# Two cross-attention layers on one Trainium2 core: projections issued in two steps, the first layer's last output chunk packed, orders and PSUM banks laid out anew

## The reference

```python
# layer 0 (its branch for tokens after the 77th is empty)
q, k, v = x @ Wq.T, ctx @ Wk.T, ctx @ Wv.T                 # split in 20 heads
x = merge(softmax(q @ k.T / 4) @ v) @ Wo.T + bo + x
# layer 1
q, k, v = x @ W_q, text @ W_k, text @ W_v                  # text: 73 tokens
p = softmax(q @ k.T / 4)
qsem = l2norm(p @ text)                                     # 512 wide, per head
sem = qsem @ l2norm(ip).T                                   # ip: 4 image tokens
p_ip = softmax(q @ k_ip.T / 4 + 0.5 * sem) * mask
x = merge(p @ v + p_ip @ v_ip) @ W_out + b_out + x
```

## Time and profile of the kernel before

| | us |
|---|---|
| median of three timed runs | 2387.35 |
| lowest and highest of them | 2387.01, 2389.14 |
| profiled execution, its own time | 2386.11 |
| profiled execution, span of the instructions | 2384.3 |
| of it, the first stage, about | 330 |
| period of the second stage | 30.76 |

### The profile page before, as it was taken

How to read it: one execution, slowest core, us unless ns; L and a number is a source line. 1 busy time by engine, 2 the same in 40 slices (tenths; PEclk the granted TensorE clock), 3 DMA queues, 4 the chain that set the end, 5 groups by cost and what they waited for, 6 DMA issues and landing times.

```text
span 2384.3 us, 85416 instructions
## 1 busy us (share of the span) xinstructions
PE 2201.3 (92%) x32824; PEld 1392.7 (58%) x32824; DVE 1832.2 (77%) x3453; ACT 1699.4 (71%) x2604; POOL 1591.4 (67%) x1056
## 2 busy tenths in 40 slices
PE   7999967999999999999999999999999999999984
PEld 5777744555555555555555555555555555555542
DVE  6856634888888888888888888888888888888873
ACT  4333316878888877888888888887888788888862
POOL 4131225777777777777777777777777777777762
PEclk9999978999999999999999999999999999999997
DMA  8877642444444444444444444444444444444431
GB/s 274 268 225 214 203 128 57 116 120 121 120 120 119 122 116 114 118 117 123 119 122 120 116 121 120 121 122 120 119 117 121 114 118 118 123 119 122 120 88 58
DMA packets 338300, 310.57 MB, mean 130 GB/s; under 512 B 180224, under 2 KB 281856, under 8 KB 337920
## 3 DMA queue, kind: packets, MB, share of 16 engines
q1 hardware_dynamic: 337920, 305.36, 45.4%
HBM read 164.66 MB, written 105.98 MB: 114 GB/s over the span
## 4 chain that ended last, share of the span: by engine, by line
PE 46%; POOL 15%; ACT 10%; issue 9%; DVE 4%; DMA 1%; SPq 0%; ACTq 0%; DVEq 0%; POOLq 0%
PE psum L1011 17%; PE psum L1096 8%; POOL e L1439 8%; ACT ef L1207 8%; PE psum L1114 8%; POOL ust L1401 5%; PE psum L1075 3%; PE psum L1014 3%; POOL al L1406 2%; PE psum L1037 2%; PE psum L1126 2%; PE psum L1051 1%; DVE x1b L1371 1%; ACT q_high L1189 1%; DVE x1a L1371 1%
## 5 line engine op out<-in xcount | busy, mean ns | idle before, releaser
L1439 POOL TENSOR_TENSOR e<-ef,eh 73x1024 f32<-73x1024 f32 x320 | 679.7, 2132 | 207.9 <-PE psum L1126 126.6
L1207 ACT ACTIVATE ef<-psum 73x1024 f32<-73x1024 f32 (+1 forms) x640 | 635.4, 1013 | 66.2 <-PE psum L1079 66.0
L1269 DVE TENSOR_REDUCE mneg<-psum 128x8 f16<-128x616 f32 (+3 forms) x512 | 451.0, 934 | 9.6 <-PE psum L1037 1.0
L1296 DVE TENSOR_TENSOR e<-psum,e 73x1024 f32<-73x1024 f32 x320 | 384.6, 1202 | 10.1 <-PE psum L1114 5.7
L1114 PE MATMUL psum<-eh,gram 128*73 128x512 f16 x1280 | 336.8, 386 | 42.8 <-DVE mneg L1269 14.3
L1096 PE MATMUL psum<-ef,values 128*32 128x256 f32 x5120 | 361.8, 387 | 0.4
L1222 ACT ACTIVATE eh<-ef 73x1024 f16<-73x1024 f32 x320 | 337.0, 1054 | 7.4
L1215 ACT ACTIVATE ust<-psum 128x512 f32<-128x512 f32 x384 | 226.5, 595 | 127.4 <-POOL al L1406 116.2
L1401 POOL TENSOR_TENSOR ust<-ust,rb 128x768 f32<-128x768 f32 x128 | 232.2, 1814 | 86.0 <-DMA rb<-r_dram 85.9
L1406 POOL TENSOR_TENSOR al<-ust,ah 128x768 f16<-128x768 f32 x128 | 210.2, 1642 | 85.8 <-ACT ah L1247 85.8
L1276 DVE SCALAR_TENSOR_TENSOR q_low<-psum,q_high 128x640 f16<-128x640 f32 x128 | 105.5, 824 | 201.6 <-ACT q_high L1189 194.5
(11 more groups left out here) (188 smaller groups left out, 4790.5 us busy)
## 6 DMA issues: line engine op xcount, KB each, us to landing
rb<-r_dram SPq DMA_DIRECT2D x128, 384.0 KB, 3.8
keys<-k_dram SPq DMA_DIRECT2D x128, 231.0 KB, 3.8
values<-v_dram SPq DMA_DIRECT2D x128, 192.5 KB
ust<-ust SPq DMA_DIRECT2D x512, 48.0 KB, 2.4
v_dram<-vst SPq DMA_DIRECT2D x64, 320.0 KB
out<-outt SPq DMA_DIRECT2D x64, 320.0 KB, 2.2
k_dram<-kst SPq DMA_DIRECT2D x32, 616.0 KB, 3.7
x<-in_x SPq DMA_DIRECT2D x32, 384.0 KB, 5.0
```

The costliest lines, as they stand in the source:

```text
L1207: act.activation(ef[l][0:m, unit_heads(n), :].rearrange("t h s -> t (h s)"), src, ACT.Exp, scale=SM).then_inc(s_exp[l], 1)
L1269: dve.tensor_reduce(dst, o, AX_X, ALU.max, negate=True).then_inc(s_max[l], 1)
L1296: dve.tensor_tensor(rest, banks(l, f"u{k}", 2)[0:m, :, :], rest, ALU.mult).then_inc(s_wr, 1)
L1439: pool.tensor_tensor(e2[0:m, k, :, :], ef[1][0:m, unit_heads(k), :], eh[0:m, unit_heads(k), :], ALU.subtract).then_inc(s_e2, 1)
```

## The change

`q` and `o` of both layers become two steps each, on all engines that touch them: part 0 is chunks 0 and 1 (512 columns, one bank), part 1 is the last chunk (128 columns, in a bank of its own). The steps need not stand together any more, and the semaphores count two per batch. Layer 0's last output chunk is packed like the others; DVE writes the two halves with two instructions, and a new SP step `xd` copies each half to the other 64 partitions with one transfer each, which POOL's `xh` of layer 1 waits for. Later steps of layer 1's output lag one batch more. `ORDER` and `USES` are written anew for all engines.

```diff
+PARTS = ((0, 1), (2,))
 ORDER = {
     "pe": """
-        1u2/3 1a1/3 0t1/1 1q/2 0t2/1 0a0/1 1s0/2 0a1/1 1s1/2 0a2/1 1i/2 1a2/3 1u3/3 1m/2 1u4/3 1t0/2 0q/0 1n0/3 1n1/3
-        1n2/3 1p/4 1u0/2 1n3/3 1n4/3 0s0/0 1a0/2 0s1/0 1u1/2 1t1/2 1o/4 1t2/2 0m/0 1y/3 0o/1 0t0/0""",
+        0a1/1 0t2/1 1q0/2 0a2/1 1s0/2 1q1/2 1a2/3 1s1/2 0q0/0 1m/2 1o1/5 1t0/2 1u4/3 1p/4 1n0/3 0s0/0 1n1/3 0q1/0
+        1t1/2 1u0/2 1n2/3 1n3/3 1n4/3 0s1/0 1o0/4 1t2/2 1u1/2 0m/0 1u2/2 1y/3 0t0/0 0o0/1 0o1/1 1u3/2 0a0/0 0t1/0 1i/2
+        1a0/2 1a1/2""",
     "act": """
-        0t0/1 0t1/1 1h4/3 1a1/3 0t2/1 1f/4 0t3/1 1q/2 0t4/1 0a0/1 1r/3 0a1/1 0a2/1 1i/2 1a2/3 1m/2 0r/1 1t0/2 1h0/2
-        1t1/2 0q/0 1h1/2 1g/4 1n/3 1a0/2 0g/1 1t2/2 1t3/2 1h2/2 1t4/2 0m/0 1h3/2""",
+        1a0/3 1i/3 1a1/3 0a1/1 1f/4 0t4/1 1q0/2 0a2/1 1q1/2 0r/0 1a2/3 1m/2 0q0/0 1t0/2 1t1/2 1h0/2 1h1/2 1g/4 0q1/0
+        1t2/2 1t3/2 1h2/2 1n/3 1h3/2 0g/1 1t4/2 0m/0 1r/3 0t0/0 0t1/0 1h4/2 0a0/0 0t2/0 0t3/0""",
     "dve": """
-        1y7/4 1y8/4 1y9/4 1y10/4 1y11/4 1w2/3 1y12/4 1y13/4 1y14/4 1y15/4 1y16/4 1y17/4 1y18/4 1ql/2 1tw0/2 1s0/2
-        1s1/2 1s2/2 1s3/2 1tw1/2 1w3/3 0d/1 1w4/3 0ql/0 1p/4 1w0/2 0s0/0 0s1/0 0s2/0 0s3/0 1w1/2 0tw0/0 1d/3 0tw1/0
-        1o/4 1y0/3 1y1/3 1y2/3 1y3/3 1y4/3 1y5/3 1y6/3 0o/1""",
+        1y9/4 1y10/4 1y11/4 1y12/4 1y13/4 1y14/4 1y15/4 1y16/4 1y17/4 1y18/4 1ql0/2 1s0/2 1s1/2 1s2/2 1s3/2 1tw0/2
+        1tw1/2 0d/1 1ql1/2 0ql0/0 1o1/5 1w4/3 1p/4 0s0/0 0s1/0 0tw0/0 1w0/2 0ql1/0 0tw1/0 0s2/0 0s3/0 1o0/4 1w1/2 1d/3
+        1y0/3 1y1/3 1y2/3 0o0/1 0o1/1 1w2/2 1y3/3 1w3/2 1y4/3 1y5/3 1y6/3 1y7/3 1y8/3""",
     "pool": """
-        1xh/2 1xl/2 1vb/4 1b3/3 0xh/0 1at/4 0xl/0 1b4/3 1c/2 1b0/2 1b1/2 1al/4 0at/1 0al/1 1b2/2 1kb/1""",
+        1xl/2 1b4/3 0xh/0 0xl/0 1at/4 1kb/2 1vb/3 1b0/2 1al/4 1c/2 0at/1 1b1/2 0al/1 1b2/2 1b3/2 1xh/1""",
     "sp": """
-        0x/0 1sh/4 1rl/4 1ps/4 1sl/3 0k/0 0ds/1 1v/2 1pl/4 1c/1 0rw/1 0sh/1 0rl/1 1ds/3 1g/1 1ns/3 1d/3 0v/0 1nl/3
-        1rw/3 1vi/2 1st/4 1ss/2 1k/1""",
+        0x/0 1ss/3 1rl/4 1ps/4 0ds/1 0k/0 1v/2 1pl/4 1c/2 1vi/2 1g/2 0rw/1 0sh/1 0rl/1 1st/5 1ds/3 1d/3 1ns/3 0v/0
+        1nl/3 1rw/3 1sl/3 0xd/1 1k/1 1sh/3""",
 }
@@
 USES = [
-    "1a1 0a0 1s2 1u3 0q 0s1 1u1 1t4",
-    "0t2 0t4 1s2 1u3 0q 0s1 1u1 1t4 0t1",
-    "0t2 0t4 1s1 1i 1u4 1n 0s2 1t2 1t4 0t1",
-    "0t3 0t4 1s1 1a2 1u4 1u0 0s2 1t2 1t4 0t0",
-    "0t3 0t4 1s0 1s3 1t0 1u0 1t3 0m 0t0",
-    "1u2 1q 1s0 1s3 1t0 1p 1a0 1t3 0o",
-    "1u2 1q 0a2 1t1 1p 0s0 0s3 1o 0o",
-    "0a1 1m 1t1 1p 0s0 0s3 1o 1y",
+    "1q0 1a2 1m 1u4 0s1 1u0 1o0 0t1 1u3 1a0",
+    "1q1 1u4 0s1 1u0 0m 0t1 1u3 1a1",
+    "0t4 1s1 1o1 1n 1t4 0t0 0a0 1i",
+    "0t4 1s1 0q0 1p 0q1 1t4 0t0 0o1 0t2",
+    "0t4 0a2 1s3 1t0 1p 1t2 0s2 1t4 1u2 0t2",
+    "0t4 1s3 1t0 1p 1t2 0s2 1t4 1u2 0t3",
+    "0a1 1s0 1s2 1t1 0s0 1t3 0s3 1u1 0o0 0t3",
+    "1s0 1s2 1t1 0s0 1t3 0s3 1u1 1y",
 ]
@@
+            def copy_tail(l, b, n):
+                b.reached(sp, s_xo[0], 2, 2)
+                tail = xin[1][b.parity()]
+                for z in (0, 1):
+                    sp.dma_start(tail[(1 - z) * HALF:(2 - z) * HALF, 2, z * TS:(z + 1) * TS],
+                                 tail[z * HALF:(z + 1) * HALF, 2, z * TS:(z + 1) * TS]).then_inc(s_xd, 16)
@@
             def query(l, b, n):
-                wait_free(pe, l, b, "q", only=0)
+                wait_free(pe, l, b, f"q{n}")
                 b.reached(pe, s_xh[l], 1, 1)
                 b.reached(pe, s_xl[l], 1, 1)
-                project(row(l, "q", 2), wqs[l], wqt[l], xh[l], xl[l], True,
-                        lambda: wait_free(pe, l, b, "q", only=1)).then_inc(f_q[l], 1)
+                project(row(l, f"q{n}"), wqs[l], wqt[l], xh[l], xl[l], PARTS[n]).then_inc(f_q[l], 1)
@@ scores
                 if c == 0:
-                    b.reached(pe, s_qh[l], 1, 1)
+                    b.reached(pe, s_qh[l], 2, 1)
@@ high_input
-                b.reached(pool, (s_x, s_xo[0])[l], (16, 1)[l], (16, 1)[l])
+                b.reached(pool, (s_x, s_xd)[l], (16, 32)[l], (16, 32)[l])
```

More of the change, by code:

```diff
@@ L832, in row, with part @@
             return banks(l, use, n).rearrange("p r n -> p (r n)")
+        def part(n):
+            return slice(PARTS[n][0] * S, (PARTS[n][-1] + 1) * S if n == 0 else PW)
         def wait_free(eng, l, b, *uses, only=None):
@@ L996, in _, with project @@
         def _(pe):
[L997 to L1002, removed]
+            def project(o, w, tail, high, low, chunks):
+                for at_chunk, c in enumerate(chunks):
+                    halves = c == 2
                     cols = slice(c * P, c * P + (HALF if halves else P))
@@ L1060, in turned_scores @@
                 if c == 0:
-                    b.reached(pe, s_ql[l], 1, 1)
+                    b.reached(pe, s_ql[l], 2, 1)
                     b.reached(pe, s_tw[l], 2, 2)
                     b.reached(pe, s_mt[l], 1, 1)
+                if c == 2:
+                    b.reached(pe, s_ql[l], 2, 2)
                 for e in range(2):
@@ L1156, in output @@
             def output(l, b, n):
-                wait_free(pe, l, b, "o", only=0)
+                wait_free(pe, l, b, f"o{n}")
                 b.reached(pe, s_al[l], 1, 1)
-                project(row(l, "o", 2), wos[l], wot[l], ah[l], al[l], l == 1,
-                        lambda: wait_free(pe, l, b, "o", only=1)).then_inc(f_o[l], 1)
+                project(row(l, f"o{n}"), wos[l], wot[l], ah[l], al[l], PARTS[n]).then_inc(f_o[l], 1)
             def softmax_turn(l, b, n):
@@ L1184, in query @@
                 b.reached(act, f_t[l], CW, 0)
-                b.reached(act, s_ql[l], 1, 0)
+                b.reached(act, s_ql[l], 2, 0)
                 if l:
                     b.reached(act, f_i, 1, 0)
-                b.reached(act, f_q[l], 1, 1)
-                act.activation(qh[l][:], row(l, "q", 2)[:, 0:PW], ACT.Copy, scale=1 / WS).then_inc(s_qh[l], 1)
+                b.reached(act, f_q[l], 2, n + 1)
+                cols = part(n)
+                act.activation(qh[l][:, cols], row(l, f"q{n}")[:, 0:cols.stop - cols.start], ACT.Copy,
+                               scale=1 / WS).then_inc(s_qh[l], 1)
             def turn_max(l, b, n):
@@ L1274, in query_rests @@
                     b.reached(dve, f_i, 1, 0)
-                b.reached(dve, s_qh[l], 1, 1)
-                dve.scalar_tensor_tensor(ql[l][:], row(l, "q", 2)[:, 0:PW], 1 / WS, qh[l][:], ALU.mult, ALU.subtract)\
-                   .then_inc(s_ql[l], 1)
+                b.reached(dve, s_qh[l], 2, n + 1)
+                cols = part(n)
+                dve.scalar_tensor_tensor(ql[l][:, cols], row(l, f"q{n}")[:, 0:cols.stop - cols.start], 1 / WS,
+                                         qh[l][:, cols], ALU.mult, ALU.subtract).then_inc(s_ql[l], 1)
             def twins(l, b, e):
                 b.reached(dve, f_t[l], CW, 0)
-                b.reached(dve, s_qh[l], 1, 1)
+                b.reached(dve, s_qh[l], 2, 2)
                 dve.stream_shuffle(twin[l][:, e, :], qh[l][:].bitcast(I32), TWIN[e]).then_inc(s_tw[l], 1)
@@ L1368, in output @@
                     b.reached(dve, s_store, 16, -16)
-                b.reached(dve, f_o[l], 1, 1)
-                dst, n = (xin[1][b.parity()][:].rearrange("p c s -> p (c s)"), CW * S) if l == 0 else (outt[:, b.parity(), :], PW)
-                dve.scalar_tensor_tensor(dst, row(l, "o", 2)[:, 0:n], 1 / WS, res[l][:, b.parity(), :], ALU.mult,
-                                         ALU.add).then_inc(s_xo[l], 1)
+                b.reached(dve, f_o[l], 2, n + 1)
+                cols = part(n)
+                src = row(l, f"o{n}")[:, 0:cols.stop - cols.start]
+                if l:
+                    ins = dve.scalar_tensor_tensor(outt[:, b.parity(), cols], src, 1 / WS, res[l][:, b.parity(), cols], ALU.mult,
+                                                   ALU.add)
+                elif n == 0:
+                    ins = dve.scalar_tensor_tensor(xin[1][b.parity()][:, 0:2, :].rearrange("p c s -> p (c s)"), src, 1 / WS,
+                                                   res[l][:, b.parity(), cols], ALU.mult, ALU.add)
+                else:
+                    for z in (0, 1):
+                        rows, mine = slice(z * HALF, (z + 1) * HALF), slice(2 * S + z * TS, 2 * S + (z + 1) * TS)
+                        ins = dve.scalar_tensor_tensor(xin[1][b.parity()][rows, 2, z * TS:(z + 1) * TS], src[rows, :], 1 / WS,
+                                                       res[l][rows, b.parity(), mine], ALU.mult, ALU.add)
+                ins.then_inc(s_xo[l], 1)
             program("dve", {"s": maxima, "ql": query_rests, "tw": twins, "d": inverses, "w": weighted, "y": ip_softmax,
```

31 lines of the change are left out of this document (16 added, 15 removed).

## The result

| | before | after |
|---|---|---|
| median of the runs, us | 2387.18 | 2494.98 |
| lowest and highest | 2386.35, 2389.14 | 2488.48, 2502.04 |
| profiled execution, its own time | 2386.11 | 2502.04 |
| its span | 2384.3 | 2500.2 |
| first to last `pip` of layer 1 (63 periods) | 434.6 to 2365.2: 30.64 each | 440.2 to 2480.8: 32.39 each |

After is slower by 4.5%: ratio 1.0446, 95% interval 1.0432 to 1.046. That is 108 us where 18 were forecast, outside the range. Of the 115.9 us between the spans, 110.0 lie in the 63 periods and 5.6 ahead of the first `pip`, where the pipeline fills (the longer lag of some steps, which the forecast left at nothing).

What follows compares the result with a forecast made beforehand. PE was taken as the bound: 28.7 us of steps − 0.3 for packing + 2.64 of waits gave 31.04 us a period against 30.76, +17 us over 62 periods, so a median of 2405 us; range 2362 to 2432.

Steps and rivals of the forecast that it cites:

- The copies cost nothing in this sum, on account of this cover: From 0o0, the copies' path to xl's end takes 9.05 us, PE's steps to 1q0 9.15: 0.1 us of cover.
- The sum: PE's period: 28.7 − 0.3 + 2.64 = 31.04 us against 30.76, so +0.28 a period, +17 us over 62.
- The rival of the copy's path: SP reaches 0xd 0.8 us late, delaying xh, xl and 1q0 (by 0.7): period 31.7, 2446 us; chance 0.12.
- The packed chunk: Layer 0's output on PE falls from 2.72 to 2.42 us: −0.30 us a period, −19 us in all.
- The split's cost on DVE and ACT: More instructions add 0.8 us a period on DVE, to 26.0, and 0.36 on ACT, to 25.2; neither the bound.
- Points 1 and 2: PE waits at 1s0 for ACT's q_high, 0.43 us; then for DVE's maxima, 0.67, and twins at 1t0, 0.19.
- Point 3: On PE, 1p takes 1t0's banks and waits 0.3 us a period for an exponential, a new wait.
- Points 4 and 6: PE waits for DVE's reads at 0q1 and 1t1, 0.2 us each, and at 1i for ACT's read, 0.15.
- Point 5: Chain from 0d through SP's spread, POOL's at, ACT's g and 1t4's exponential makes 1u2 on PE wait 0.3 us.
- PE sets the pace: PE bounds the kernel: busy 29.34 of 30.76 us a period, the next engine with 5.5 us less work.

Runs made afterwards that it cites:

- e9: Kernel before with only the split: projections in two steps, old lists and banks, layer 0's last output chunk unpacked, no copies; 2373.6 us, ratio 0.9936.
- e10: e7 with layer 0's last output chunk unpacked and the copies left out; 2418.3 us, ratio 1.0123.
- e7: e5 with 1n0 put ahead of 1p on PE; 2427.6 us, ratio 1.0175.
- e2: Kernel after with layer 0's input load (0x) ahead of the four moves 1sh, still behind the copies and keys; 2440.8 us, ratio 1.0236.
- e3: Kernel after with layer 0's last output chunk unpacked and no copies; 2436.1 us, ratio 1.0203.
- e6: e2 with layer 1's two query steps next to each other on PE and ACT; 2440.3 us, ratio 1.0208.
- e5: e2 with layer 0's four moves ahead of its inverses' store on SP, and 1c and 1vi behind 0rl; 2432.6 us, ratio 1.0185.
- e12: e9 with layer 0's two output banks exchanged and DVE reading part 0 only when part 1 is there too; 2374.7 us, ratio 0.9948.
- e4: Kernel before with only layer 0's last output chunk packed and its two copies added, old orders and banks; 2650.6 us, ratio 1.1112.
- e1: Kernel after with layer 0's input load (0x) issued ahead of the copies, the keys and the four moves; 2448.3 us, ratio 1.0253.
- e8: Kernel after with layer 0's input load (0x) pushed further back on SP, behind the store 1ss; 2680.0 us, ratio 1.1212.

## Why the prediction was wrong, by its steps

The medians (some of them from different chips) divide the loss as follows: split −16 us (before to e9, its own comparison), new lists, banks and lags +45 (e9 to e10), packing with its copies +9 (e10 to e7), places of the moves and of 1n0 +13 (e7 to e2), the input's load behind the moves +54 (e2 to after); together +105 of 108. The parts are not independent. Without the copies the load's place, the moves' and 1n0's are worth 18 us together (e3 to e10), with them 67 (after to e7): the load is late because SP is held by the copies *and* the moves stand between.

- **The step that failed: "The copies cost nothing in this sum, on account of this cover".** The cover was worked out for one transfer, the copy, and one consumer, 1q0. That part was even right: in the period shown `xl` of layer 1 ends at 1251.32 and 1q0 starts at 1251.98, 0.66 us of cover for the 0.1 forecast. Missing was what stands *behind* a waiting instruction on its own queue: the copies' 1.2 us of issue, the keys, the moves with 2.5 to 3.8, then 0x with a landing for which the page of before gave 5.0 us. In the period shown that adds up to 12.24 us from DVE's write to 0q0. In e2, where PE doesn't wait for `xl`, PE itself takes 11.55 from 0o1's end to 0q0 (1190.25 to 1201.80), of which 10.7 lie behind DVE's write (done at 1191.08). The path is 1.5 us too long. Averaged from SP's first copy to 0q0 it is 12.03 us in after and 10.70 in e2; the row of PE's waits, 26.8 us in 600, is 1.45 a period. The forecast listed the new order of SP without laying it out in time, as it had done for PE.
- **The sum would have failed without this step too.** e2, free of the wait, is at 2440.8, above the range's upper end of 2432. The forecast's +0.28 us a period was −0.30 of work and +0.59 of waiting; by windows from 1000 to 1600 us, PE in e2 is busy for 29.25 us a period and idle for 2.30, against 29.35 and 1.42 before: −0.10 and +0.88. So the new order takes back 0.2 of what packing saves, and waits 0.3 more than forecast, though the waits listed in e2 (2.0 a period) stay under the forecast's 2.64.
- **The rival of the copy's path** was the nearest (2446, at 0.12), but had the wrong victim and stopped at a price of 0.7 us a period. Its sign, "POOL's `xh` waiting over 2 us", is there; the PE wait with it is another step's.
- **The packed chunk:** right, 2.42 us. Worth less than its transfers all the same (e10 against e7).
- **The split's cost on DVE and ACT:** busy times right (26.2 and 25.3), the effect of the wrong sign: e9 gains. The forecast counted only work added, not that a reader may start one chunk sooner.
- **Points 1 and 2:** right in place. `q_high` 0.40 each (0.43 forecast), the maxima 4.2 and 3.6 us in 19 periods of e2, 0.41 together for 0.67 (in after the wait for `xl` covers them); and by e6 the one stands behind the other. A wait for the twins (0.19) is not listed.
- **Point 3,** 1p for an exponential: rare (3.9 us in 7 of 18 periods), and where it is gone, the probabilities' load takes its place, which was not forecast.
- **Points 4 and 6:** no such wait is listed in after or in e2.
- **Point 5:** the chain is there, and L1126's wait hangs on it (e5), but 0.7 us a time in e2 and up to 2.1, for the 0.3 forecast. Which of the chain's terms was too small was not read.
- **Not forecast:** 0t1 waits for the weighted product (L1087, 0.2 us a period), and the fill takes 5.6 us more.
- **"PE sets the pace"** was too simple already. The chain of before had PE at 46% and POOL and ACT at 25% together; e12 shows a PE wait of 0.43 us a period that costs 0.02.

Still open: e10 has listed waits of 1.36 us a period (26.1 in 600 us) and before 1.24 (24.1), yet its period is 0.40 longer. By windows half of that is PE busy for longer (29.56 us a period, for 29.35 before, at granted clock 1.00 in both) and half is idle time (1.62 for 1.42). Which steps take the one, and what the small idle pieces wait for, no run tells. What the new lists gain or lose one by one (PE's, ACT's, DVE's) wasn't tried beyond e5 to e7.

## What to carry to other kernels

When a transfer that waits for a result is put into an in-order queue, lay that queue out in time up to the next transfer that does *not* depend on the result, and add its landing and its consumer: its victim need not be the one that the transfer was made for (here it was 0q0 in after, and 1q in e4). A load of a later batch belongs in front of the step that waits or close behind it; here either place removed the wait at 0q0 (e1, e2). And before an edit is costed by the wait it adds or removes on the busiest engine, look at the chain of waits: where another engine sets that stretch, as ACT does in e12, the wait can be free.

## What the hardware showed that I had not expected

A wait of PE can cost more than its length. After 1.76 us of waiting 0q0's sixteen products run at the full rate, 1258.38 to the transposes at 1260.12; after 2.09 us at the next 0q0 they begin at it and fall in the middle, so that the transposes come 2.64 us after the start:

```profile
1290.62 0.60 PE L1022 MATMUL psum<-xh,wq 128*128 128x256 f16 x4 [2.09 <-POOL xl L1421]
...
1291.55 1.06 PE L1022 MATMUL psum<-xh,wq 128*128 128x256 f16 x4
...
1293.26 0.42 PE L1061 MATMUL psum<-ident,mneg 128*128 128x128 f16 x2
```

```profile
1290.60:1293.40 2.80, 2.78 (x18) 2.16 (x18) 1.53 (x7) 0.00 (x0) 2.23 (x2) 0.64 0.28 67
1258.30:1260.30 2.00, 1.92 (x18) 1.69 (x18) 2.00 (x6) 0.00 (x0) 2.00 (x2) 1.00 0.42 120
```

The granted clock is 0.64 over the first stretch, so most of it is at the lower of the two levels, 1.2 GHz, and 1.00 over the second. In e4 one projection takes 3.15 us after a wait of 2.79, and another 1.84 after one of 2.81; the length of the wait alone does not decide. How often it happens grows with the waits: 6 of 19 times at 0q0 in after (PE's wait 1.45 us a period), every time in e8 (3.6 a period). The Trainium skill describes in "TensorE: Matmul & The Clock Gate", HAM oscillation, a kernel whose waits for transfers drop the clock at *every* tile; here it is some of them. Over the whole span the granted clock is 0.983 before, 0.969 in after and 0.926 in e8.

Four moves of 48 KB between partitions hold SP for 3.72 us in the chain shown, and for 2.45 in the like place of e2. Both kernels have the whole spread, 2.4 to 3.8 us in after and 2.4 to 4.0 in e2. What makes the last of the four take 1.86 instead of 0.59 us was not looked into.
